# A last group of nodes with 312 columns in place of 384, in the last stage of a graph layer and its mixture of experts

## The chip, the cores and the metric

The kernel runs on one core of one Trainium2 chip. The metric is the device time of one execution in microseconds (us); lower is better. Five engines work side by side and meet at semaphores: TensorE (PE, its weight loads shown as PEld), VectorE (DVE), ScalarE (ACT), GpSimd (POOL) and SyncE (SP), which here only issues DMAs.

## The reference

3125 nodes with 256 features pass a graph attention layer with a feed-forward block, and then a mixture of 8 experts that all see every node. The parts that the change touches are these:

```python
h = _layernorm(x + x_new, ln1_g, ln1_b)
ffn = jax.nn.gelu(h @ W1 + b1, approximate=False) @ W2 + b2      # W1 256x1024, W2 1024x256
return _layernorm(h + ffn, ln2_g, ln2_b)
...
feat = jnp.mean(x, axis=0)                     # a mean over an axis of length 1
w = jax.nn.softmax(feat @ Wr + br, axis=-1)    # a weight for each node and expert
h = jnp.einsum('bfd,edh->bfeh', x, W1) + b1
h = jax.nn.relu(_bn(h, g1, be1, m1, v1))
h = jnp.einsum('bfeh,ehk->bfek', h, W2) + b2
h = jax.nn.relu(_bn(h, g2, be2, m2, v2))
y = jnp.einsum('bfeh,ehd->bfed', h, Wo) + bo
return jnp.einsum('bfed,fe->bfd', y, w)
```

## The kernel before

The program has three parts, run one after the other: `project` (keys, values, queries), `attend` (the graph attention, some 880 us of the span), and `tail` (line numbers from about 1040), which holds the feed-forward and the experts. Only `tail` is touched.

The nodes lie in NB = 25 blocks of BP = 128 rows. 24 blocks are full, and the last holds REST = 53 real nodes; its other rows are padding. `tail` takes the blocks in NC = 7 groups of CH = [3, 4, 4, 4, 4, 3, 3] blocks, numbered 0 to 6; group 6, the last, holds the partly filled block. A group of 4 blocks is 512 columns wide when the features lie on the partitions, a group of 3 blocks 384.

Each float32 product is made of three products of rounded float32 parts (type fp32r): high by low, low by high, high by high. With the contraction over 256 features in KC = 2 halves this is 6 matmuls for one 128-wide slice of the output. Two shapes of product occur:

- The nodes as the moving operand, the weights stationary. These are the feed-forward's first product (`hidden_first`, L1509, L1510, L1512: 8 slices `m` for each group, so 48 matmuls) and the experts' layers 1 and 2 (`layer`, L1554, L1555, L1557: 2 slices for each, so 12 matmuls for each layer, group and expert). They stream as many columns as the group has: `cols(g)`.
- The nodes stationary, the weights moving. These are the feed-forward's second product (`hidden_second`, L1532 to L1534), the experts' third layer (`third`, L1572, L1573, L1575), the bias product (`biases`, L1586 to L1588) and the router (`router`, L1485, L1488). They work block by block; the first three stream 256 columns, the router 16 or 8.

Behind each product with moving nodes stands a chain of three engines. ACT reads PSUM and applies Gelu (L1374, and L1375 for the rounded high part) or scale, bias and Relu (`hidden`, L1386); DVE makes the rounded high part in the experts' layers (L1786); POOL subtracts to get the low part (`gelu_low` L1279, `hidden_low` L1287). All of them work on `cols(g)` columns. PE needs the low part before it can use the result in the next product.

The order on each engine is written out by hand. In the experts' loop a step `i` from 0 to NJ - 1 = 55 is one expert and one group (`e, g = i // NC, i % NC`), and PE does `layer(1, i + 1)`, `layer(2, i)`, and then `third(i - 1)`, so that each chain has another step's products to hide behind. Some late work of the last group of the feed-forward is put between the steps (`LATE_X`, `LATE_R`), and the bias products of the 7 groups are spread over steps 9 to 15. DVE adds each expert's output, weighted, into the result (`combined`, L1801). The output of a group goes out by DMA (L1254, L1257) when its last expert is added.

Of the kernel before, what the change touches and what calls it, by code (L numbers as in the profile page):

```python
# [29 lines left out]
N, HID, E = 3125, 256, 53125  # L30
H, D = 4, 64
FF = 4 * HID
NB, BP = 25, 128
NPAD = NB * BP
FULL = N // BP
REST = N - FULL * BP
# [25 lines left out]
CH = [3, 4, 4, 4, 4, 3, 3]  # L62
NC = len(CH)
NPT = NC * FC
S_LAG = 2
NE = 8
XP = [(0, 4), (4, 12), (12, 20), (20, NB)]
EV = TP // 16 * 16
PARTS = [(0, REST // 16 * 16), (REST // 16 * 16, REST)]
SGRP = [(0, 4), (4, 8), (8, 12), (12, 16), (16, 20), (20, NB)]  # L70
KVB = 4
QEARLY = 9
# [18 lines left out]
def project(nc, ctx, io, keep):  # L91

    c = ExitStack()
    with c:
# [92 lines left out]
        def _(sp):  # L187
            def piece(k):
                a, b = XP[k]
                sp.dma_start(xs[:, a:min(b, FULL), :], x_v[:, a:min(b, FULL), :]).then_inc(s_x[k], 16)  # L190
                if b > FULL:
                    sp.wait_ge(s_pad, 3)
                    for a, b in PARTS:
                        sp.dma_start(xs[a:b, FULL, :], x_r[a:b, :]).then_inc(s_x[k], 16)
# [36 lines left out]
        def _(pool):  # L231
# [14 lines left out]
            def roots(k):  # L246
                a, b = SGRP[k]
                pool.wait_ge(s_mv, b)
                nc.gpsimd.tensor_scalar(ve[:, a:b], mv[:, a:b, 1], LN_EPS, None, ALU.add).then_inc(s_ve, 1)
                pool.wait_ge(s_ve, k + 1)  # L250
                nc.gpsimd.tensor_tensor(rs[:, a:b], ve[:, a:b], mh[:, a:b], ALU.pow).then_inc(s_rs, 1)
# [119 lines left out]
        def _(dve):  # L371
# [14 lines left out]
            def arrived(t):  # L386
                for k, (a, b) in enumerate(XP):
                    if t == a:
                        dve.wait_ge(s_x[k], 16 + 16 * len(PARTS) if b > FULL else 16)

            def norm(t):
                for k, (a, b) in enumerate(SGRP):
                    if t == a:
                        dve.wait_ge(s_rs, k + 1)
                if t >= 4:
                    dve.wait_ge(s_tr, t - 3)
                nc.vector.tensor_scalar(xn[:, t % 4, :], xs[:, t, :], mv[:, t, 0:1], rs[:, t:t + 1],
                                        ALU.subtract, ALU.mult).then_inc(s_xn, 1)
# [646 lines left out]
def tail(nc, ctx, io, keep):  # L1045

    c = ExitStack()
    with c:
        def sb(name, shape, dt=F32):
            return c.enter_context(nc.sbuf_tensor(name, shape, dt))  # L1050

        def pb(name, shape):
            return c.enter_context(nc.psum_tensor(name, shape, F32))
# [6 lines left out]
        xh = sb("xh", [P, KC, NPAD], F32R)  # L1060
        xl = sb("xl", [P, KC, NPAD], F32R)
# [37 lines left out]
        wrs = sb("wrs", [P, KC, 2 * NE], F32R)  # L1099
# [9 lines left out]
        psT = pb("psT2", [P, 512])  # L1109
# [23 lines left out]
        def size(g):  # L1133
            return CH[g]

        def first(g):
            return sum(CH[:g])

        def cols(g):
            return CH[g] * BP  # L1140

        def blocks(g):
            return slice(first(g), first(g) + size(g))
# [58 lines left out]
        def _(sp):  # L1202
# [5 lines left out]
            def inputs(g):  # L1208
# [4 lines left out]
                if g == NC - 1:  # L1213
                    for a, b in PARTS:
                        sp.dma_start(xin[a:b, full, :], x_r[a:b, :]).then_inc(s_xin, 16)
# [35 lines left out]
            for g in range(NC):  # L1251
# [3 lines left out]
                if g == NC - 1:  # L1255
                    for a, b in PARTS:
                        sp.dma_start(out_r[a:b, :], acc[a:b, NB - 1, 0:HID]).then_inc(s_out, 16)  # L1257
            sp.wait_ge(s_out, 16 * NC + 16 * len(PARTS))

# [184 lines left out]
        def _(pe):  # L1444
            def bank_free(use):

                n = t_at[use]
                if n:
                    before = T_USES[n - 1]
                    if before[0] in "TX":  # L1450
                        pe.wait_ge(s_th, tx_at[before] + 1)
                    else:
                        pe.wait_ge(s_pd, td_at[before] + 1)
# [23 lines left out]
            def router(g):  # L1477
                bank_free(("R", g))
                if g == 0:
                    pe.wait_ge(s_wrs, 4)  # L1480
                pe.wait_ge(s_tl, tx_at["X", g, KC - 1] + 1)
                for u in range(size(g)):
                    t = (first(g) + u) * BP
                    for k in range(KC):
                        nc.tensor.matmul(psT[:, 2 * NE * u:2 * NE * (u + 1)], xh[:, k, t:t + BP], wrs[:, k, :],  # L1485
                                         start=(k == 0), stop=False)
                    for k in range(KC):
                        last = nc.tensor.matmul(psT[:, 2 * NE * u:2 * NE * u + NE], xl[:, k, t:t + BP], wrs[:, k, 0:NE],  # L1488
                                                start=False, stop=(k == KC - 1))
                last.then_inc(s_pt, 1)  # L1490

# [68 lines left out]
            def third(i):  # L1560
                e, g = i // NC, i % NC
                pe.wait_ge(s_gl, low_at["L2", i, 1] + 1)
                if g == 0:
                    pe.wait_ge(s_wl, 3 * e + 3)
                hi, lo = half(e, 2, 0), half(e, 2, 1)
                for b, pair in enumerate(banks(g)):
                    ps = output_free(("L3", i, b))
                    for u in pair:
                        out = ps[:, (u % 2) * HID:(u % 2 + 1) * HID]
                        at = slice(u * BP, (u + 1) * BP)  # L1570
                        for k in range(KC):
                            nc.tensor.matmul(out, h2h[:, i % 2, k, at], lo[:, k, :], start=(k == 0), stop=False)  # L1572
                            nc.tensor.matmul(out, h2l[:, i % 2, k, at], hi[:, k, :], start=False, stop=False)  # L1573
                        for k in range(KC):
                            last = nc.tensor.matmul(out, h2h[:, i % 2, k, at], hi[:, k, :], start=False, stop=(k == KC - 1))  # L1575
                    last.then_inc(s_o, 1)

            def biases(g):

                pe.wait_ge(s_pd, td_at["wT", g] + 1)  # L1580
                for b, pair in enumerate(banks(g)):
                    ps = output_free(("bias", g, b))
                    for u in pair:
                        out = ps[:, (u % 2) * HID:(u % 2 + 1) * HID]
                        at = slice(u * BP, (u + 1) * BP)
                        nc.tensor.matmul(out, wTh[:, g % 2, at], bol[:, :], start=True, stop=False)  # L1586
                        nc.tensor.matmul(out, wTl[:, g % 2, at], boh[:, :], start=False, stop=False)
                        last = nc.tensor.matmul(out, wTh[:, g % 2, at], boh[:, :], start=False, stop=True)  # L1588
                    last.then_inc(s_o, 1)
# [14 lines left out]
            for p in range(NPT):  # L1604
                g, m = p // FC, p % FC
# [5 lines left out]
                if m == 4 and g == 1:  # L1611
                    bank_free(("sc",))
                    pe.wait_ge(s_sc, 6)
                    for k in range(4):
                        last = nc.tensor.transpose(psT[:, k * NP:(k + 1) * NP], sc[:, k, :], ident[0:NP, 0:NP])
# [28 lines left out]
        def _(dve):  # L1644
            def rows(t, n):
                return t[:, :].unsqueeze(1).broadcast_to([BP, n, HID])
# [54 lines left out]
            def second_stats(g):  # L1701
# [16 lines left out]
                last.then_inc(s_c2, 1)  # L1718
                dve.wait_ge(s_xin, 16 * g + 16 + (16 * len(PARTS) if g == NC - 1 else 0))
                nc.vector.tensor_tensor(xin[:, 0:n, :], xin[:, 0:n, :], rows(be2, n), ALU.add).then_inc(s_xb, 1)  # L1720
# [271 lines left out]
```

## Time and profile before

| | |
|---|---|
| time, median of 3 runs | 1502.57 us (1501.42 to 1509.48) |
| profiled execution, its own time | 1504.69 us |
| profiled execution, span from first to last instruction | 1502.9 us |
| mean granted TensorE clock over the span | 0.933 |
| PE, DVE, ACT, POOL busy over the span | 83%, 72%, 54%, 62% |

The span is 1.8 us shorter than the execution's own time, which also holds what lies around the first and the last instruction. The page cuts the span into 40 equal slices of 37.6 us; `tail` begins in the 24th. From the 29th slice on nearly every slice has the digit 9 for PE, that is 90% or more. A matmul's duration in the trace includes its way through the array, and overlaps the next one's: how fast PE gets on is read from the distance between the starts, not from the durations. Where the idle time of an engine is given, the arrow names what ended it.

### The profile page before, as it was taken

The numbers are of one execution on the slowest core, as the hardware profiler recorded it, in microseconds if no ns is written. First come the engines' busy times: TensorE is split into PE (matmuls) and PEld (weight loads), VectorE is DVE, ScalarE is ACT, GpSimd is POOL, SyncE is SP. The second block draws the span as 40 slices with busy tenths as digits, with TensorE's granted clock in tenths as the row PEclk, the third lists the DMA queues.
The fourth block names the chain that finished last, engine by engine and source line by source line (L and its number), as shares of the span: only waits on it lengthen the run. The fifth ranks groups of instructions, "written<-read, shape, count | busy, mean of one in ns | idle before, by whom it ended". The sixth has DMA issues, their size and how long they took to land. (4 is left out here: it accounts for less than half of the span.)

```text
span 1502.9 us, 24128 instructions
## 1 busy us (share of the span) xinstructions
PE 1247.5 (83%) x6835; PEld 966.9 (64%) x6835; DVE 1078.1 (72%) x2557; ACT 810.3 (54%) x2534; POOL 930.9 (62%) x883
## 2 busy tenths in 40 slices
PE   7988776677767677667657889999999999999998
PEld 3444454454445444444445578889898899999998
DVE  7647877777777787777868779886766665656655
ACT  1356766556666766566657654565543344444443
POOL 3365566656666665666665556866765477667765
PEclk9999879888898898998988999999999999999999
DMA  7477766666666666666665120101000000000002
GB/s 222 162 218 210 224 192 192 178 180 185 199 186 199 178 199 174 201 172 197 184 180 166 31 75 29 52 27 40 9 15 22 1 22 15 8 22 15 1 12 76
DMA packets 74072, 175.40 MB, mean 117 GB/s; under 512 B 11500, under 2 KB 36651, under 8 KB 73945
## 3 DMA queue, kind: packets, MB, share of 16 engines
q0 software_dynamic: 37632, 124.28, 29.6%
q1 hardware_dynamic: 34641, 48.25, 9.6%
q10 hardware_dynamic: 1672, 1.33, 0.3%
q8 instruction: 61, 1.00, 0.3%
q14 instruction: 66, 0.54, 0.1%
HBM read 159.91 MB, written 13.91 MB: 116 GB/s over the span
## 5 line engine op out<-in xcount | busy, mean ns | idle before, releaser
L690 POOL DMA_INDIRECT ring<-kv_rows,idx x464 | 466.5, 1005 | 296.4 <-issue 116.6
L764 ACT ACTIVATE ring<-ring 128x64 f32<-128x64 f32 x1800 | 442.1, 336 | 17.2 <-issue 16.1
L1287 POOL TENSOR_TENSOR wm<-k_gf,wm 128x512 fp32r<-128x512 f32 (+1 forms) x224 | 264.0, 1181 | 147.1 <-DVE wm L1786 147.1
L1386 ACT ACTIVATE k_gf<-psF,k_scT 128x512 f32<-128x512 f32 (+1 forms) x224 | 164.0, 733 | 258.3 <-PE psF L1557 258.3
L1786 DVE CAST wm<-k_gf 128x512 fp32r<-128x512 f32 (+1 forms) x224 | 168.8, 758 | 158.7 <-ACT k_gf L1386 157.0
L810 PE MATMUL psA<-ring,oh 128*128 128x260 f32 x912 | 274.1, 429 | 7.5 <-DVE k_acc L1016 7.1
L784 PE MATMUL psQ<-k_q,ohT 128*128 x1392 | 225.3, 304 | 58.7 <-issue 58.2
L982 DVE TENSOR_TENSOR prod<-psQ,ring 128x512 f32<-128x512 f32 x232 | 157.4, 678 | 89.5 <-remote 59.9
L784 PEld LDWEIGHTS psQ<-k_q,ohT 128*128 128x128 bf16 x1392 | 131.9, 105 | 115.7 <-issue 86.0
L810 PEld LDWEIGHTS psA<-ring,oh 128*128 128x128 f32 x912 | 178.0, 217 | 36.5 <-issue 8.5
L1022 DVE TENSOR_REDUCE alpha<-prod 128x8 f32<-128x512 f32 x232 | 155.6, 671 | 0.2
L1016 DVE TENSOR_TENSOR k_acc<-k_acc,psA 128x260 f32 x232 | 93.6, 403 | 15.4 <-PE psA L810 12.3
L1279 POOL TENSOR_TENSOR gT<-k_gf,gT 128x512 fp32r<-128x512 f32 (+1 forms) x56 | 74.1, 1325 | 38.8 <-ACT gT L1375 38.7
L1801 DVE SCALAR_TENSOR_TENSOR k_acc<-psO,wt,k_acc 128x256 f32<-128x256 f32 x200 | 84.8, 473 | 9.4 <-PE psO L1575 9.3
L1000 DVE TENSOR_TENSOR oh<-k_iotaF,k_dstR 128x256 f32<-128x256 f32 x217 | 88.3, 407 | 0.0
L1374 ACT ACTIVATE k_gf<-psF,b1c 128x512 f32<-128x512 f32 (+1 forms) x56 | 36.0, 642 | 77.3 <-PE psF L1512 77.2
L1532 PE MATMUL psO<-wm,gT 128*128 128x256 f32 x200 | 58.9, 294 | 0.0
L749 ACT ACTIVATE nrow<-psM 64x128 f32<-64x128 f32 x29 | 7.8, 270 | 93.4 <-remote 43.7
L1534 PE MATMUL psO<-wm,gT 128*128 128x256 f32 x200 | 57.0, 285 | 0.0
L1533 PE MATMUL psO<-wm,gT 128*128 128x256 f32 x200 | 56.9, 285 | 0.0
L846 PE MATMUL psA<-k_wqs,k_acc 128*128 128x512 f32 x100 | 49.3, 617 | 8.0 <-ACT qst L715 4.0
L755 ACT ACTIVATE ring<-dif 128x64 f32<-128x64 f32 x29 | 9.7, 334 | 85.6 <-DVE dif L961 60.8
(284 smaller groups left out, 2671.9 us busy)
## 6 DMA issues: line engine op xcount, KB each, us to landing
ohT<-step_destinations SPq DMA_DIRECT2D x29, 512.0 KB
ring<-kv_rows,idx POOLq DMA_INDIRECT x464
kv_rows<-kvst SPq DMA_DIRECT2D x25, 260.0 KB, 2.4
we<-in_L_ffn_W SPq DMA_DIRECT2D x16, 256.0 KB, 2.8
residual<-qst SPq DMA_DIRECT2D x25, 128.0 KB
xs<-in_x SPq DMA_DIRECT2D x2, 1024.0 KB, 8.8
resin<-residual SPq DMA_DIRECT2D x4, 512.0 KB
we<-in_L_ffn_Wo SPq DMA_DIRECT2D x8, 256.0 KB, 2.7
```

What stands on the lines that cost most here:

```text
L690: nc.gpsimd.indirect_dma_start(out=ring[:, LT * (j % CP) + k, j // CP:j // CP + 2, :].rearrange("p t e -> p (t e)"), out_offset=None, in_= ...
L764: last = nc.scalar.activation(row[:, 0:D], row[:, 0:D], ACT.Copy, scale=row[:, D:HW_])
L784: last = nc.tensor.matmul(psQ[j % NQ][:, k * HID:(k + 1) * HID], ohT[par][:, w * P:(w + 1) * P], q3[:, part, bass.ds(blk, 1), :].rearrange ...
L810: last = nc.tensor.matmul(psA[sj % NA][0:BP, 0:HALFW], onehot(b, k), ring[:, LT * (sj % CP) + k, sj // CP, :], start=(k == 0), stop=(k == ...
L982: nc.vector.tensor_tensor(prod[:, j % 2, :].rearrange("p (k d) -> p k d", k=LT), psQ[j % NQ][:, :].rearrange("p (k d) -> p k d", k=LT), ri ...
L1000: nc.vector.tensor_tensor(oh[:, sj % NO, :, :], iotaF[:, 0:BP].unsqueeze(1).broadcast_to([P, LT, BP]), dstR[:, bass.ds(LT * bo, LT)].unsqu ...
L1016: nc.vector.tensor_tensor(row, row, psA[sj % NA][0:BP, 0:HALFW], ALU.add).then_inc(s_acc, 1)
L1022: nc.vector.tensor_reduce(alpha[:, q % 2, :, LT * jj:LT * jj + LT].rearrange("p h w -> p w h"), prod[:, j % 2, :].rearrange("p (k h d) -> ...
L1287: nc.gpsimd.tensor_tensor(low[:, i % 2, m, 0:w], gf[:, n % 4, 0:w], high[:, i % 2, m, 0:w], ALU.subtract).then_inc(s_gl, 1)
L1386: nc.scalar.activation(gf[:, n % 4, 0:cols(g)], ps, ACT.Relu, bias=bias, scale=scale).then_inc(s_ev, 1)
L1786: nc.vector.tensor_copy((h1h if layer == 1 else h2h)[:, i % 2, m, 0:w], gf[:, n % 4, 0:w]).then_inc(s_dh, 1)
L1801: last = nc.vector.scalar_tensor_tensor(out=x1(t), in0=psO[n % 3][:, (u % 2) * HID:(u % 2 + 1) * HID], scalar=wt[:, t, e:e + 1], in1=x1(t) ...
```

## The change

The last group is narrower: its third block counts RC = 56 columns (53 rounded up to a multiple of 8) in place of 128, so `cols(6)` is 2 x 128 + 56 = 312 in place of 384, for every instruction that uses `cols(g)` on PE, ACT, DVE and POOL. In the router, the third layer and the bias product of the last block, 56 rows are stationary in place of 128, and 56 PSUM partitions are written. The feed-forward's second product still takes three blocks of 128 stationary rows, and the transposes, `combined` and the DMAs are as before.

```diff
--- before.py
+++ after.py
@@ -67,6 +67,7 @@
 XP = [(0, 4), (4, 12), (12, 20), (20, NB)]
 EV = TP // 16 * 16
 PARTS = [(0, REST // 16 * 16), (REST // 16 * 16, REST)]
+RC = -(-REST // 8) * 8
 SGRP = [(0, 4), (4, 8), (8, 12), (12, 16), (16, 20), (20, NB)]
 KVB = 4
 QEARLY = 9
@@ -1137,7 +1138,10 @@
             return sum(CH[:g])
 
         def cols(g):
-            return CH[g] * BP
+            return CH[g] * BP if g < NC - 1 else (CH[g] - 1) * BP + RC
+
+        def rows_in(g, u):
+            return RC if g == NC - 1 and u == CH[g] - 1 else BP
 
         def blocks(g):
             return slice(first(g), first(g) + size(g))
@@ -1480,12 +1484,12 @@
                     pe.wait_ge(s_wrs, 4)
                 pe.wait_ge(s_tl, tx_at["X", g, KC - 1] + 1)
                 for u in range(size(g)):
-                    t = (first(g) + u) * BP
+                    t, n = (first(g) + u) * BP, rows_in(g, u)
                     for k in range(KC):
-                        nc.tensor.matmul(psT[:, 2 * NE * u:2 * NE * (u + 1)], xh[:, k, t:t + BP], wrs[:, k, :],
+                        nc.tensor.matmul(psT[0:n, 2 * NE * u:2 * NE * (u + 1)], xh[:, k, t:t + n], wrs[:, k, :],
                                          start=(k == 0), stop=False)
                     for k in range(KC):
-                        last = nc.tensor.matmul(psT[:, 2 * NE * u:2 * NE * u + NE], xl[:, k, t:t + BP], wrs[:, k, 0:NE],
+                        last = nc.tensor.matmul(psT[0:n, 2 * NE * u:2 * NE * u + NE], xl[:, k, t:t + n], wrs[:, k, 0:NE],
                                                 start=False, stop=(k == KC - 1))
                 last.then_inc(s_pt, 1)
 
@@ -1566,8 +1570,9 @@
                 for b, pair in enumerate(banks(g)):
                     ps = output_free(("L3", i, b))
                     for u in pair:
-                        out = ps[:, (u % 2) * HID:(u % 2 + 1) * HID]
-                        at = slice(u * BP, (u + 1) * BP)
+                        n = rows_in(g, u)
+                        out = ps[0:n, (u % 2) * HID:(u % 2 + 1) * HID]
+                        at = slice(u * BP, u * BP + n)
                         for k in range(KC):
                             nc.tensor.matmul(out, h2h[:, i % 2, k, at], lo[:, k, :], start=(k == 0), stop=False)
                             nc.tensor.matmul(out, h2l[:, i % 2, k, at], hi[:, k, :], start=False, stop=False)
@@ -1581,8 +1586,9 @@
                 for b, pair in enumerate(banks(g)):
                     ps = output_free(("bias", g, b))
                     for u in pair:
-                        out = ps[:, (u % 2) * HID:(u % 2 + 1) * HID]
-                        at = slice(u * BP, (u + 1) * BP)
+                        n = rows_in(g, u)
+                        out = ps[0:n, (u % 2) * HID:(u % 2 + 1) * HID]
+                        at = slice(u * BP, u * BP + n)
                         nc.tensor.matmul(out, wTh[:, g % 2, at], bol[:, :], start=True, stop=False)
                         nc.tensor.matmul(out, wTl[:, g % 2, at], boh[:, :], start=False, stop=False)
                         last = nc.tensor.matmul(out, wTh[:, g % 2, at], boh[:, :], start=False, stop=True)
```

No instruction is added, removed or moved on any engine; on PE 240 instructions change from 384 to 312 columns (48 of the feed-forward, 192 of the experts), and 55 from 128 to 56 rows. The end of PE's program shows both. `psF` holds a layer's result, `wm` the activations, `gT` the weights, `psO` the output of the third layer; the piece is the second slice of layer 2 of the last step, and then the beginning and the end of what follows. Before:

```order
L1554 MATMUL psF<-wm,gT 128x384
L1555 MATMUL psF<-wm,gT 128x384
L1554 MATMUL psF<-wm,gT 128x384
L1555 MATMUL psF<-wm,gT 128x384
L1557 MATMUL psF<-wm,gT 128x384 x2
L1572 MATMUL psO<-gT,wm 128x256
...
L1572 MATMUL psO<-gT,wm 128x256
L1573 MATMUL psO<-gT,wm 128x256
L1575 MATMUL psO<-gT,wm 128x256 x2
```

The same rows after the change (lines are 4 to 5 further down in the file):

```order
L1558 MATMUL psF<-wm,gT 128x312
L1559 MATMUL psF<-wm,gT 128x312
L1558 MATMUL psF<-wm,gT 128x312
L1559 MATMUL psF<-wm,gT 128x312
L1561 MATMUL psF<-wm,gT 128x312 x2
L1577 MATMUL psO<-gT,wm 128x256
...
L1577 MATMUL psO<-gT,wm 56x256
L1578 MATMUL psO<-gT,wm 56x256
L1580 MATMUL psO<-gT,wm 56x256 x2
```

The places and the count are the same; only the moving width of the layer and the output rows of the last block differ.

## Rows read from the trace of the kernel before

**Rows 1.** The page: busy time by engine, and busy tenths in 40 slices.
```profile
PE 1247.5 (83%) x6835; PEld 966.9 (64%) x6835; DVE 1078.1 (72%) x2557; ACT 810.3 (54%) x2534; POOL 930.9 (62%) x883
PE   7988776677767677667657889999999999999998
```

**Rows 2.** Busy time by stretch: from:to, length, PE, PEld, DVE, ACT, POOL, clock, DMA.
```profile
1030.00:1051.50 21.50, 21.44 (x159) 21.04 (x158) 12.45 (x29) 12.52 (x25) 14.72 (x14) 1.00 0.15 44
1087.00:1091.00 4.00, 4.00 (x23) 4.00 (x23) 2.00 (x4) 2.22 (x5) 3.63 (x4) 0.61 0.02 8
1150.00:1156.00 6.00, 6.00 (x26) 5.46 (x25) 2.32 (x6) 1.44 (x3) 1.96 (x3) 0.72 0.16 44
1156.00:1200.00 44.00, 43.60 (x277) 39.39 (x276) 30.25 (x53) 13.38 (x19) 21.86 (x20) 1.00 0.03 7
1200.00:1494.00 294.00, 294.00 (x1789) 272.35 (x1788) 177.49 (x297) 122.88 (x172) 202.06 (x171) 1.00 0.06 18
```

**Rows 3.** PE in order of time, groups 5 and 6 of one expert: start, duration.
```profile
1328.02 0.34 PE L1554 MATMUL psF<-xh,ew 128*128 128x384 f32 x1
...
1332.19 0.28 PE L1572 MATMUL psO<-ew,wm 128*128 128x256 f32 x1
...
1335.06 0.34 PE L1554 MATMUL psF<-xh,gT 128*128 128x384 f32 x1
```

**Rows 4.** All engines in order of time, a stretch of 512 columns.
```profile
1462.11 0.39 PE L1554 MATMUL psF<-xh,gT 128*128 128x512 f32 x1
...
1466.19 0.28 PE L1572 MATMUL psO<-gT,wm 128*128 128x256 f32 x1
```

**Rows 5.** PE in order of time, the last group of the feed-forward, slices 1 and 2.
```profile
1032.30 0.34 PE L1509 MATMUL psF<-hT,wm 128*128 128x384 f32 x1
...
1034.41 0.34 PE L1509 MATMUL psF<-hT,wm 128*128 128x384 f32 x1
```

**Rows 6.** Waits after 1087 us: who for whom, us in total, times, longest.
```profile
PE psT L1474 <- ACT xn L1355: 3.6, 1, 3.6
PE psO L1572 <- POOL wm L1287: 0.4, 1, 0.4
```

**Rows 7.** All engines in order of time, the last step.
```profile
1494.44 0.67 ACT L1386 ACTIVATE k_gf<-psF,k_scT 128x384 f32<-128x384 f32 x1 [0.37 <-PE psF L1557]
1495.14 0.63 DVE L1786 CAST wm<-k_gf 128x384 fp32r<-128x384 f32 x1 [0.68 <-ACT k_gf L1386]
1495.86 1.01 POOL L1287 TENSOR_TENSOR wm<-k_gf,wm 128x384 fp32r<-128x384 f32 x1 [0.29 <-DVE wm L1786]
1496.15 0.40 PE L1575 MATMUL psO<-gT,wm 128*128 128x256 f32 x2
1496.92 0.39 PE L1572 MATMUL psO<-gT,wm 128*128 128x256 f32 x1 [0.38 <-POOL wm L1287]
```

**Rows 8.** Groups by line and shape after 800 us: busy us, mean ns, idle before.
```profile
L1287 POOL TENSOR_TENSOR wm<-k_gf,wm 128x512 fp32r<-128x512 f32 x128 | 166.6, 1303 | 88.1 <-DVE wm L1786 88.1
L1786 DVE CAST wm<-k_gf 128x512 fp32r<-128x512 f32 x128 | 101.6, 797 | 101.9 <-ACT k_gf L1386 101.9
L1386 ACT ACTIVATE k_gf<-psF,k_scT 128x512 f32<-128x512 f32 x128 | 99.6, 779 | 152.1 <-PE psF L1557 152.1
L1287 POOL TENSOR_TENSOR wm<-k_gf,wm 128x384 fp32r<-128x384 f32 x96 | 97.4, 1017 | 59.0 <-DVE wm L1786 59.0
L1786 DVE CAST wm<-k_gf 128x384 fp32r<-128x384 f32 x96 | 67.3, 706 | 56.8 <-ACT k_gf L1386 55.1
L1386 ACT ACTIVATE k_gf<-psF,k_scT 128x384 f32<-128x384 f32 x96 | 64.4, 672 | 106.2 <-PE psF L1557 106.2
```

**Rows 9.** PE in order of time, the router's last block of the last group.
```profile
1102.43 0.37 PE L1485 MATMUL psT<-wrs,xh 128*128 128x16 f32 x2
1102.65 0.36 PE L1488 MATMUL psT<-wrs,xl 128*128 128x8 f32 x2
1102.88 0.42 PE L1554 MATMUL psF<-wm,ew 128*128 128x384 f32 x1
```

## The prediction

> **What bounds the kernel now.** I read the page first. PE has the largest busy share, and its row of tenths is 9 in nearly every slice from the 29th on [rows 1]; before that no engine fills its slices, but the change touches nothing there. So I went to busy time by stretch. In the experts' steady part, 1200 to 1494 us, PE is busy 294.00 of 294.00 us at a granted clock of 1.00, while DVE has 177.49, ACT 122.88 and POOL 202.06 [rows 2]. In the stretch that holds the feed-forward's last group, 1030 to 1051.5 us, PE is busy 21.44 of 21.5 us, again at clock 1.00 [rows 2]. Both places in which the change shortens PE's work are bound by PE alone. The view of waits agrees: of PE's waits that end after 1087 us two matter here, 3.6 us before the transposes of the feed-forward's last group, which end at its left edge, and 0.4 us for POOL at the very end [rows 6].
>
> Since durations overlap, I took the price of a matmul from the distance of starts. Width 384: 24 matmuls from 1328.02 to 1332.19 us, 4.17 / 24 = 173.8 ns. Width 256: 24 from 1332.19 to 1335.06, 2.87 / 24 = 119.6 ns [rows 3]. Width 512: 18 from 1462.11 to 1466.19, 4.08 / 18 = 226.7 ns [rows 4]. The three lie on a line: 54.2 ns and 52.9 ns for 128 columns more, in the mean 0.418 ns for a column (one column in a cycle of the upper clock level, 2.4 GHz, would be 0.417), and about 13 ns that don't depend on the width.
>
> **The change part by part.**
>
> *Layers 1 and 2 of the experts, on PE.* 8 experts x 2 layers x 12 matmuls = 192, each 72 columns shorter: 72 x 0.418 = 30.1 ns, from 173.8 to 143.7 ns. Sum 5.78 us. The four-block and other three-block groups are unchanged.
>
> *First product of the feed-forward, on PE.* 48 matmuls x 30.1 ns = 1.44 us. Is it on the path? From one slice to the next are 1034.41 - 1032.30 = 2.11 us [rows 5]; 6 matmuls of 384 and 9 of 256 make 6 x 173.8 + 9 x 119.6 = 2.12 us. There is no gap, so all of it counts. ACT, DVE and POOL are busy 12.5, 12.5 and 14.7 of these 21.5 us [rows 2], and their pieces for this group shrink with PE's, so none becomes the bound.
>
> *The chain behind each product.* ACT, DVE and POOL shorten too: from 512 to 384 columns their means fall 107, 91 and 286 ns [rows 8], so 72 columns less are 60, 51 and 161 ns. In the loop this is worth nothing, because PE's other products hide the chain. It counts once: in the last step PE has only `third` of step 54 to hide behind, runs out of it, and waits. Its last two matmuls start at 1496.15, so the next could start at 1496.15 + 2 x 0.12 = 1496.39; it starts at 1496.92, behind ACT 0.67, DVE 0.63 and POOL 1.01 us [rows 7]. The stall of 0.53 us shrinks by 60 + 51 + 161 ns = 0.27 us, and 0.26 us stay. What is late next is still POOL's low part. Bounds: 0.16 us (POOL alone) to 0.53 us (the stall gone).
>
> *56 stationary rows in the router.* Here the moving operand has only 16 or 8 columns, and still the last block's 4 matmuls take from 1102.43 to 1102.88, 0.45 / 4 = 112 ns each [rows 9]: at such widths the weight load of 128 columns is the price. With 56 columns I take 112 x 56 / 128 = 49 ns, saving 4 x 63 = 0.25 us, once. No row shows a load of 56 columns; the bounds are 0 and 0.25 us, and I take 0.2, as it would scale with columns.
>
> *56 stationary rows in the third layer and the bias product.* 8 x 6 + 3 matmuls. Their start distance is 119.6 ns, above the 112 ns of a full load [rows 3, 9], so the moving 256 columns set it. I take 0. Below, if the 13 ns that don't depend on width belong to the load and scaled with its columns, 51 x 13 x 72 / 128 = 0.4 us would be saved; above, nothing suggests more than 0.1 us lost.
>
> *Everything else.* The transposes' copies, wT and the last group's Gelu pieces are shorter off the path. The wait of 3.6 us [rows 6] hangs on DVE and ACT work of 256 features for each block, which is unchanged; it moves with PE and stays as long.
>
> Sum: 5.78 + 1.44 + 0.27 + 0.20 = 7.7 us. Against the profiled execution's own time, 1504.69 us, this gives 1497.0 us. That execution lies 2.1 us above the median of the three runs, so against the median of 1502.57 us it gives 1494.9 us, 0.51% less.
>
> A rule of the Trainium skill speaks against this size: "TensorE: Matmul & The Clock Gate", section "Back-to-back issue gap", gives for a sustained stream of loads and matmuls about 81 ns at 128 columns and 131 ns at 512, so 0.13 ns for a column. By that rule 240 matmuls would save only 240 x 72 x 0.13 = 2.3 us as an estimate. The trace does not agree: 226.7 ns at 512 columns.
>
> **The rivals.**
>
> *The clock falls more often (the one on the other side).* PE's clock is granted by what PE has done. The trace has a stretch at the lower level, 1.2 GHz, that follows no long wait: 1150 to 1156 us has a mean clock of 0.72 [rows 2], behind bias products with few rows and transposes. It cost (1 - 0.72) x 6 = 1.7 us. If the third layer's last block, with 56 of 128 stationary columns, did the same after each pass of the last group, 8 x 1.7 = 13.4 us would be lost, and the time would be 1502.6 - 7.7 + 13.4 = 1508.3 us; with twice that for each pass, 1522. It decides from 7.7 / 1.7 = 5 passes on. For it: bias products are narrow in the array too. Against it: in the steady part, which holds such a block every seventh step, the clock is 1.00 throughout, the narrow part would be 6 matmuls or 0.7 us among hundreds at full size, and the later bias products, from 1156 to 1200 us, left the clock at 1.00 [rows 2].
>
> *Part of the gain is given back, or one low stretch more.* If the feed-forward's share were taken up by a wait for POOL's chain, 1.4 us less is won: 1496.4 us. One more stretch at the lower level (1.7 us) gives 1496.6 us, and both with the end's stall unchanged and the router's term at nothing 1494.9 + 1.4 + 1.7 + 0.5 = 1498.5 us. For it: after the long wait the clock is 0.61 for 4 us [rows 2], and where such a stretch falls depends on what stands around it, which moves by 1.4 us. Against it: ACT, DVE and POOL have 7 to 9 us of slack in 21.5.
>
> *One low stretch less.* By the same shift the stretch at 1150 us may fall away: 1494.9 - 1.7 = 1493.2 us.
>
> *Widths that are no multiple of 128 don't follow the line.* No row shows a width between 256 and 384 for these products. If 312 cost as much as 384, only the end and the router stay: 1502.1 us. If the cost for a column were much smaller there, as the rule above has it, 2.3 + 0.5 us are won: 1499.8 us. The three widths on one line, at one column in a cycle, speak against both.
>
> **How the numbers follow.** Chances: the forecast 0.71 (own range 1492.3 to 1497.5, which is one low stretch and the scatter of the medians), partly given back 0.14, one low stretch less 0.07, off the line 0.03, more low stretches 0.05. The time is that of the forecast, 1494.9 us. Eight in ten reach over the forecast's range and most of the two cases beside it: 1491.2 to 1499.6 us. About 0.5% (7.5 us) is what a measurement of this kernel can tell from no change, and the forecast lies just past this line, so it is split: 0.45 of its 0.71 is beyond it, 0.26 within. Faster by over 0.5%: 0.45 + 0.07 = 0.52. Within 0.5%: 0.26 + 0.14 + 0.03, and 0.02 of the slower rival at one stretch a pass, makes 0.45. Slower by over 0.5%: 0.03.
>
> **What the profile of the changed kernel would show.** The step of one expert is shorter by 24 x 30 ns = 0.72 us every 7 steps; width 312 has a start distance of 144 ns. From slice to slice in the feed-forward's last group are 1.94 us. The last stall of PE is near 0.3 us. The router's last 4 matmuls come at about 50 ns. PE's busy share from 1200 us on stays at all of it, at clock 1.00. The prediction is wrong if that distance is not 144 ns, if PE begins to wait in the loop for POOL or DVE, or if the mean clock behind the passes of the last group falls below 1.00.

## The result, and the profile after

| | before | changed |
|---|---|---|
| median, 9 runs each | 1502.57 us (1498.76 to 1509.48) | 1492.04 us (1487.78 to 1499.95) |
| ratio of the runs | | 0.9947 (0.9924 to 0.9969) |
| profiled execution, its own time | 1504.69 us | 1499.95 us |
| its span | 1502.9 us | 1498.1 us |

The forecast was 1494.9 us with a ratio of 0.995. The median of 1492.04 us lies 0.3 us below the forecast's own range (1492.3 to 1497.5) and inside the wider one (1491.2 to 1499.6). Two later comparisons, each of 12 runs of the changed kernel with 23 and 19 of the kernel before, gave 0.9951 (0.9916 to 0.9985) and 0.9937 (0.9914 to 0.9960).

The times scatter by some 20 us, and the traces say where: before the part that was changed (three traces of the changed kernel come into it at 1014.64, 1024.46 and 1035.40 us, and take 458.9 to 459.0 us from there). The stretch that the change touches runs from the first matmul of the feed-forward's last group to the last matmul of the program. I call it the tail below; it is only the last part of what the function `tail` does. In the kernel before, PE in order of time (start, duration) at its two ends:

```profile
1030.12 0.38 PE L1509 MATMUL psF<-hT,wm 128*128 128x384 f32 x1
...
1498.94 0.40 PE L1575 MATMUL psO<-gT,wm 128*128 128x256 f32 x2
```

The last matmul of the pair starts at 1499.06, so the tail is 468.94 us. The same for the changed kernel:

```profile
1035.40 0.31 PE L1513 MATMUL psF<-hT,wm 128*128 128x312 f32 x1
...
1494.20 0.40 PE L1580 MATMUL psO<-gT,wm 128*56 128x256 f32 x2
```

Its last matmul starts at 1494.32: 458.92 us. The tail is 10.0 us shorter, while this execution came into it 5.3 us later, by work that no edit touched. So the trace shows the change a good deal more sharply than the times do. 10.0 us are a ratio of 0.9933, inside all three intervals.

Busy time by stretch in the changed kernel (from:to, length, PE, PEld, DVE, ACT, POOL, clock, DMA), to compare with [rows 2]:

```profile
1035.00:1056.50 21.50, 21.30 (x167) 21.01 (x166) 11.67 (x29) 11.83 (x26) 13.95 (x15) 1.00 0.18 52
1090.70:1095.00 4.30, 4.30 (x26) 4.30 (x27) 2.22 (x4) 2.31 (x5) 3.94 (x5) 0.67 0.05 18
1152.00:1158.00 6.00, 5.93 (x33) 5.20 (x33) 3.56 (x8) 2.02 (x3) 2.77 (x3) 1.00 0.13 44
1158.00:1200.00 42.00, 42.00 (x275) 37.98 (x275) 28.91 (x53) 12.55 (x19) 21.39 (x20) 1.00 0.03 7
1200.00:1487.00 287.00, 287.00 (x1769) 265.40 (x1769) 168.96 (x294) 120.92 (x171) 197.50 (x170) 1.00 0.06 18
```

PE is still the only bound in the steady part. What is new is the third row: the stretch with a clock of 0.72 that stood at 1150 us in [rows 2] is not there. The widths themselves, in PE's order of time, beside [rows 3]:

```profile
1335.19 0.30 PE L1558 MATMUL psF<-wm,ew 128*128 128x312 f32 x1
...
1336.90 0.28 PE L1577 MATMUL psO<-ew,wm 128*128 128x256 f32 x1
```

12 matmuls in 1.71 us are 142.5 ns each; the forecast was 143.7. The router's last block, beside [rows 9]:

```profile
1105.99 0.25 PE L1489 MATMUL psT<-wrs,xh 128*56 128x16 f32 x2
1106.09 0.24 PE L1492 MATMUL psT<-wrs,xl 128*56 128x8 f32 x2
1106.19 0.42 PE L1558 MATMUL psF<-wm,ew 128*128 128x384 f32 x1
```

4 matmuls in 0.20 us, 50 ns each in place of 112. And the last step, beside [rows 7]:

```profile
1489.97 0.61 ACT L1390 ACTIVATE k_gf<-psF,k_scT 128x312 f32<-128x312 f32 x1 [0.24 <-PE psF L1561]
1490.62 0.59 DVE L1792 CAST wm<-k_gf 128x312 fp32r<-128x312 f32 x1 [0.53 <-ACT k_gf L1390]
1491.29 0.85 POOL L1291 TENSOR_TENSOR wm<-k_gf,wm 128x312 fp32r<-128x312 f32 x1 [0.26 <-DVE wm L1792]
1491.69 0.40 PE L1580 MATMUL psO<-gT,wm 128*128 128x256 f32 x2
1492.19 0.38 PE L1577 MATMUL psO<-gT,wm 128*128 128x256 f32 x1
```

From 1491.69 + 0.24 = 1491.93 to 1492.19 PE stalls for 0.26 us; before it was 0.53.

Every instruction has the same place in both programs, so the tails can be laid side by side, matmul by matmul. A low stretch is one in which the granted clock is at its lower level. This is where the 10.0 us come from:

| part of the tail | forecast | measured |
|---|---|---|
| experts' layers 1 and 2, width | 5.78 | 5.68 |
| feed-forward's first product, width | 1.44 | 1.42 |
| router, 56 rows | 0.20 | 0.24 |
| end of the last chain | 0.27 | 0.28 |
| low stretch near 1150 us gone | a rival, 1.7 | 1.54 |
| waits and starts in the bias products | 0 | 0.87 |
| sum | 7.7 | 10.03 |

### The profile page after: what moved, and what is told of

Same layout as the page of the kernel before. It is cut to its first block and busy times, and to the rows that moved or that the text cites. A ratio compares the mean times of both kernels' runs of the same rounds, so it can differ in the third digit from the quotient of the medians.

```text
span 1498.1 us, 24128 instructions
## 1 busy us (share of the span) xinstructions
PE 1242.9 (83%) x6835; PEld 959.2 (64%) x6835; DVE 1068.4 (71%) x2557; ACT 807.4 (54%) x2534; POOL 927.2 (62%) x883
## 5 line engine op out<-in xcount | busy, mean ns | idle before, releaser
L1291 POOL TENSOR_TENSOR wm<-k_gf,wm 128x512 fp32r<-128x512 f32 (+2 forms) x224 | 258.9, 1159 | 144.1 <-DVE wm L1792 144.1
L1390 ACT ACTIVATE k_gf<-psF,k_scT 128x512 f32<-128x512 f32 (+2 forms) x224 | 162.1, 724 | 252.2 <-PE psF L1561 248.9
L785 PE MATMUL psQ<-k_q,ohT 128*128 x1392 | 228.6, 305 | 60.7 <-issue 56.0
L1792 DVE CAST wm<-k_gf 128x512 fp32r<-128x512 f32 (+2 forms) x224 | 159.5, 719 | 155.8 <-ACT k_gf L1390 155.8
L1283 POOL TENSOR_TENSOR gT<-k_gf,gT 128x512 fp32r<-128x512 f32 (+2 forms) x56 | 73.3, 1310 | 38.2 <-ACT gT L1379 38.1
L1378 ACT ACTIVATE k_gf<-psF,b1c 128x512 f32<-128x512 f32 (+2 forms) x56 | 35.5, 634 | 76.9 <-PE psF L1516 76.8
L1578 PE MATMUL psO<-ew,wm 128*128 128x256 f32 (+1 forms) x200 | 52.9, 286 | 0.0
```

The lines of the kernel that those rows point to most:

```text
L785: last = nc.tensor.matmul(psQ[j % NQ][:, k * HID:(k + 1) * HID], ohT[par][:, w * P:(w + 1) * P], q3[:, part, bass.ds(blk, 1), :].rearrange ...
L1291: nc.gpsimd.tensor_tensor(low[:, i % 2, m, 0:w], gf[:, n % 4, 0:w], high[:, i % 2, m, 0:w], ALU.subtract).then_inc(s_gl, 1)
L1390: nc.scalar.activation(gf[:, n % 4, 0:cols(g)], ps, ACT.Relu, bias=bias, scale=scale).then_inc(s_ev, 1)
L1792: nc.vector.tensor_copy((h1h if layer == 1 else h2h)[:, i % 2, m, 0:w], gf[:, n % 4, 0:w]).then_inc(s_dh, 1)
```

## The experiments

Length of the tail in every profiled kernel, in us. Where a low stretch stands near the bias products, the last column says how far behind the start of the tail it begins. w192 and third_56_all leave out a part of the result.

| kernel | tail | low stretch near the bias products |
|---|---|---|
| before, first / again | 468.94 / 468.93 | at 121.4 / at 149.6 |
| changed, first / again / third | 458.92 / 458.92 / 458.99 | no / no / no |
| rows_only | 468.47 | at 121.3 |
| pe_only | 460.52 | no |
| experts_only | 460.20 | no |
| ffn_only | 469.19 | at 121.7 |
| third_56_all | 459.22 | at 118.1 |
| early_norm | 462.78 | at 121.7 |
| early_norm_late_router | 460.04 | no |
| w192 | 454.96 | no |
| rc54 | 458.77 | no |

### before_again and after_again: what is scatter

No edit.

> The kernel before once more, as a control for the scatter. Theory (the gain is the width on PE, the rest is scatter): ratio to the kernel before 1.000 with an interval of about 0.3% to either side; in the trace the same start distances (173.8 ns at 384 columns) and the end's stall of 0.53 us, but the stretches at the lower clock may lie elsewhere, one more or less (1.7 us each) behind 1026 us. Rival (the low stretch at 1150 us belongs to the kernel before): a low stretch at 1145 to 1160 us again.

Measured: ratio to the kernel before 1.0002 (0.9975 to 1.0030). The tail is the same to 0.01 us, though this execution came into it 16 us earlier. The low stretch is there again, but behind another bias product, 28 us further on. Busy time by stretch and, below it, the bias product just before it, all engines in order of time:

```profile
1163.00:1169.00 6.00, 6.00 (x23) 4.94 (x22) 1.69 (x4) 1.70 (x3) 1.28 (x1) 0.72 0.01 3
```

```profile
1159.16 1.02 POOL L1287 TENSOR_TENSOR wm<-k_gf,wm 128x384 fp32r<-128x384 f32 x1 [0.30 <-DVE wm L1786]
1159.23 1.17 DVE L1786 CAST wm<-k_gf 128x384 fp32r<-128x384 f32 x1
...
1160.89 0.55 DVE L1821 TENSOR_TENSOR hT<-psT,hT 8x384 fp32r<-8x384 f32 x1
1160.89 0.38 PE L1586 MATMUL psO<-bol,hT 8*128 8x256 f32 x1
...
1161.36 1.25 DVE L1801 SCALAR_TENSOR_TENSOR k_acc<-psO,wt,k_acc 128x256 f32<-128x256 f32 x3
...
1162.27 0.38 PE L1586 MATMUL psO<-bol,hT 8*128 8x256 f32 x1 [0.40 <-DVE k_acc L1801]
```

The second row is the one to look at. DVE's cast of 384 columns lasts 1.17 us here, where 0.36 us is its shortest; it began 0.07 us after POOL's subtraction and ended only behind it. DVE is thereby late with adding the expert's output, which frees the bank that the bias product waits for. That is the 0.4 us wait of PE (0.66 us with the slower start behind it). In the first trace of the kernel before the same cast lasts 1.16 us and the wait is the same, but the low stretch begins 28 us ahead of the wait: the two need not go together.

> The changed kernel once more. Theory: ratio 0.995 (7.7 us), interval about 0.992 to 0.998; in the trace from the feed-forward's last group on, the same 30 ns for each of 240 matmuls, and low stretches behind the feed-forward at places that differ from the first trace's. Rival (the change itself takes away the low stretch at 1150 us): none there again, and a ratio nearer 0.994.

Measured: 0.9951 (0.9916 to 0.9985), tail 458.92 us, no low stretch near the bias products. So the rival's sign came and the ratio was the theory's, though an interval this wide cannot part 0.995 from 0.994. At the same place in the changed kernel's first trace:

```profile
1176.27 1.00 POOL L1291 TENSOR_TENSOR wm<-k_gf,wm 128x384 fp32r<-128x384 f32 x1 [0.30 <-DVE wm L1792]
1176.35 1.33 DVE L1792 CAST wm<-k_gf 128x312 fp32r<-128x312 f32 x2 [0.16 <-ACT k_gf L1390]
...
1177.54 1.68 POOL L1291 TENSOR_TENSOR wm<-k_gf,wm 128x312 fp32r<-128x312 f32 x2 [0.26 <-DVE wm L1792]
...
1178.66 1.24 DVE L1807 SCALAR_TENSOR_TENSOR k_acc<-psO,wt,k_acc 128x256 f32<-128x256 f32 x3
...
1178.94 0.38 PE L1592 MATMUL psO<-bol,hT 8*128 8x256 f32 x1
```

Two casts now begin before POOL's next subtraction. The first is still held until the subtraction beside it ends (1.10 us), and the second begins in the gap between two of them and takes 0.31 us. DVE starts its adding 0.28 us before the bias product's first matmul (1178.94) instead of 0.47 us behind it (1161.36 against 1160.89), and the wait is gone. Shorter casts are not needed for that: in pe_only they have 384 columns and the wait is gone too. What counts is when they begin.

### rows_only: the 56 rows alone

```diff
         def cols(g):
-            return CH[g] * BP if g < NC - 1 else (CH[g] - 1) * BP + RC
+            return CH[g] * BP
```

> Only the rows: 384 columns everywhere as before, but 56 stationary rows for the last block in the router, the third layer and the bias product. Theory: the router's last 4 matmuls fall from 112 to about 50 ns (0.25 us in all), the third layer's last 6 stay at 119 to 120 ns, nothing else moves; the time is within 0.5 us of the kernel before, scatter aside. Rival (narrow products lower the clock): low stretches appear after passes of the last group, 1.7 us each, up to 13 us.

Measured: tail 468.47 us, 0.47 less than before. The router gives 0.24 of it, matmuls at 50 ns; the rest lies in single intervals under 0.1 us. No low stretch is added behind the passes of the last group; the one near the bias products stays. The rival on the other side has nothing to stand on here.

### pe_only: the helpers keep 384 columns

```diff
         def cols(g):
+            return CH[g] * BP
+
+        def pcols(g):
             return CH[g] * BP if g < NC - 1 else (CH[g] - 1) * BP + RC
...
-                    h1h[:, i % 2, :, 0:cols(g)], h1l[:, i % 2, :, 0:cols(g)])
+                    h1h[:, i % 2, :, 0:pcols(g)], h1l[:, i % 2, :, 0:pcols(g)])
...
-                    ps = product_free(f_at[f"L{l}", i, m])[:, 0:cols(g)]
+                    ps = product_free(f_at[f"L{l}", i, m])[:, 0:pcols(g)]
```

Likewise in `hidden_first`.

> 312 columns on PE alone; ACT, DVE and POOL still work on 384 of them (the last 72 are left over from other work and used by nobody that is kept). Theory: the whole of the layers' gain, 24 x 30 = 0.72 us for each expert and 8 x 6 x 30 = 1.44 us in the feed-forward, but the stall at the end stays at about 0.53 us instead of 0.27. Rival (the helpers' shorter work carries part of the gain): the step of one expert shrinks by clearly less than 0.7 us, as PE begins to wait for ACT or POOL in the loop.

Measured: tail 460.52 us, 1.60 more than the changed kernel. In the experts' loop the intervals are the changed kernel's to some hundredths of a us, but for those around the long wait, so the helpers carry nothing there. The end's last interval is 0.45 us longer (forecast 0.27). The rest, 1.2 us, is lost in the feed-forward's last group, which I had not expected. Waits from 1010 to 1060 us (who for whom, us in total, times, longest):

```profile
PE psT L1495 <- POOL xl L1284: 1.0, 1, 1.0
PEld psF L1519 <- ACT gT L1385: 0.6, 1, 0.6
PE psF L1519 <- POOL hT L1284: 0.5, 1, 0.5
PEld psO L1542 <- POOL gT L1289: 0.4, 1, 0.4
```

PE waits for ACT and POOL there. (The two waits at L1519 end with the tail's first matmul and are not in its length.) The helpers' 384 columns need not be the cause. In twelve of the fourteen traces a low stretch slows PE in the 20 us ahead of the tail. pe_only and early_norm_late_router alone have none, and they alone wait for POOL's low part before the router here for more than 0.23 us: 1.0 us, and 0.6 us with the helpers at 312 columns. Busy time by stretch for those 20 us, in pe_only and in the changed kernel:

```profile
990.80:1010.80 20.00, 18.22 (x134) 17.63 (x135) 17.81 (x39) 10.80 (x23) 15.10 (x12) 1.00 0.00 1
```

```profile
1015.40:1035.40 20.00, 18.90 (x130) 18.45 (x129) 15.61 (x42) 9.46 (x21) 13.46 (x13) 0.91 0.08 21
```

So a PE that was not slowed comes to this group ahead of its helpers. That this makes most of the 1.2 us is argued from two traces, and the helpers' widths may add to it: this stays open.

### experts_only and ffn_only: the two halves

`cols(g)` is split into one for the feed-forward and one for the experts; one of them is 384 for the last group.

```diff
+        def fcols(g):
+            return CH[g] * BP
...
-                x0, x1 = hTh[:, g % 2, :, 0:cols(g)], hTl[:, g % 2, :, 0:cols(g)]
+                x0, x1 = hTh[:, g % 2, :, 0:fcols(g)], hTl[:, g % 2, :, 0:fcols(g)]
```

> 312 columns in the experts alone; the feed-forward's first product and its helpers keep 384. Measured from the start of the feed-forward's last group to the last matmul (468.94 us in the kernel before, 458.92 us in the changed one). Theory (each part counts by itself, and the bias product's wait and the low stretch near it belong to the experts' widths): 458.92 + 1.4 = 460.3 us, no wait of 0.66 us in the bias product, no low stretch there. Rival (the low stretch is chance, by the phase of the clock's grid): it comes back, 461.9 us.

> 312 columns in the feed-forward's first product alone; the experts keep 384 and all 128 rows. Same stretch. Theory: 468.94 - 1.4 = 467.5 us, with the bias product's wait of 0.66 us and a low stretch near the bias products as in the kernel before. Rival (chance): the low stretch is gone here too, 465.9 us.

Measured: experts_only 460.20 us, against 460.3, with neither the bias product's wait nor a low stretch. The feed-forward's first product alone is 1.44 us longer than in the changed kernel. ffn_only took 469.19 us against 467.5: the 1.4 us are there in the intervals, the wait of 0.66 us and the stretch near the bias products are back, and one more low stretch fell behind the router of group 4. Busy time by stretch of ffn_only:

```profile
906.00:912.00 6.00, 6.00 (x39) 6.00 (x39) 3.37 (x13) 1.22 (x3) 2.34 (x3) 0.72 0.64 183
1011.90:1017.90 6.00, 6.00 (x25) 5.38 (x24) 2.08 (x5) 1.64 (x3) 2.02 (x2) 0.72 0.15 44
```

The two halves are additive in their widths. What the experts' half brings beyond its widths is the wait. For the stretch one trace of each is not enough, as the next run shows.

### third_56_all: is the clock or the load sensitive to narrow products?

```diff
-                        n = rows_in(g, u)
+                        n = RC
                         out = ps[0:n, (u % 2) * HID:(u % 2 + 1) * HID]
```

in the third layer, for every block.

> The changed kernel, but in the experts' third layer every block has only 56 stationary rows, so that 72 rows of each block get no expert output. Theory (the moving 256 columns set the distance, and the clock doesn't look at how much of the array is used): 120 ns a matmul, clock 1.00 in the experts' steady part, 458.9 us. Rival (narrow products lower the clock): a third of PE's time now goes to narrow products, so the clock falls in the loop, by 1.7 us for each stretch; the stretch takes clearly over 460 us. A second rival (part of the 13 ns that no width explains belongs to the weight load): 112 to 116 ns, up to 8 us less over 1200 matmuls.

Measured: tail 459.22 us. PE in order of time, 24 narrow matmuls, and the steady part by stretch:

```profile
1180.18 0.28 PE L1577 MATMUL psO<-ew,wm 128*56 128x256 f32 x1
...
1183.04 0.34 PE L1558 MATMUL psF<-xh,gT 128*128 128x384 f32 x1
```

```profile
1050.00:1340.00 290.00, 290.00 (x1797) 266.27 (x1795) 170.98 (x298) 122.12 (x173) 198.95 (x172) 1.00 0.06 18
```

2.86 / 24 = 119.2 ns, against 119.6 ns with 128 rows, and a clock of 1.00 over 290 us in which these matmuls are near a third of PE's time. The first rival falls, and of the second's up to 8 us little is left. But not nothing: the tail holds one low stretch (1.5 us) that the changed kernel has not, and is only 0.3 us longer. The third layer's distances add up to 1.5 us less in all; in the steady part they are 0.7 ns shorter in the mean. The low stretch stands where it stood in the kernel before, though the wide groups and the bias product's wait of 0.66 us are not there.

### w192 and rc54: other widths

w192 works on 192 columns in `layer` on PE, by the edit of pe_only with 192 in place of 312 and for the experts alone, with 384 for the helpers. rc54 has 310 columns throughout:

```diff
-RC = -(-REST // 8) * 8
+RC = REST + REST % 2
```

> 192 columns in the experts' layers 1 and 2 of the last group, on PE alone; the helpers work on 384, so the columns from 192 on get left-over values. Theory (a weight load of 128 columns costs 112 ns, the router's distance in the kernel before, and can't be hidden behind less): 112 ns a matmul, not the 93.6 ns of the line through the three widths. Rival 1 (the line goes on): 93 to 94 ns. Rival 2 (narrow moving operands cost more for this type below 256 columns): clearly over 120 ns.

> The last block with 54 rows in place of 56, 310 columns. Theory (the line holds for any width): 240 x 2 x 0.418 ns = 0.20 us less than the changed kernel's 458.92, so 458.7 us, chance stretches aside. Rival (56 was chosen because other counts cost more): 143 ns a matmul or more and no gain, or DVE's casts slower than 0.36 us.

Measured in w192, PE in order of time:

```profile
1318.30 0.25 PE L1564 MATMUL psF<-wm,ew 128*128 128x192 f32 x1
...
1319.62 0.31 PE L1583 MATMUL psO<-ew,wm 128*128 128x256 f32 x1
```

1.32 / 12 = 110 ns, not the 93.6 ns of the line and not over 120: the load of 128 columns sets the distance. By an estimate from these distances the line ends where it meets 110 ns, at about 256 - (119.6 - 110) / 0.418 = 233 columns.

rc54: tail 458.77 us, 0.15 less than the changed kernel, with 0.20 expected. But the saving is not in the matmuls that became narrower. In the steady part the 24 of one expert take 1.724 + 1.711 = 3.435 us at 310 columns and 1.712 + 1.717 = 3.429 us at 312, 143 ns each in both. What is shorter is layer 2 of group 5, which follows the first twelve of them at an unchanged 384 columns: 2.083 us in place of 2.115 (2.080 in the kernel before). This is also why the table above has 5.68 us for the experts' layers: the 192 matmuls themselves save 5.93 us, and the neighbours behind them give 0.25 us back. So two columns are less than this measurement resolves, and the rival's 143 ns is what came. 54 rows are as good as 56, and no better than can be told in a time.

### early_norm, early_norm_late_router and after_third: the long wait

The changed kernel still has the 3.6 us wait [rows 6] and a low stretch behind it.

```diff
-                if i in (1, 2):
-                    root(i, NC - 1)
+                if i in (0, 1):
+                    root(i + 1, NC - 1)
...
-                if i == 1:
+                if i == 0:
                     second_stats(NC - 1)
-                if i == 2:
+                if i == 1:
                     second_norm(NC - 1)
```

> The changed kernel with the second normalisation of the feed-forward's last group one step earlier in the experts' loop on DVE and POOL (statistics in step 0, normalisation in step 1). Theory (PE's wait of 3.6 us before the transposes in step 3 and the low stretch behind it hang on DVE's order): the wait goes, and with it the low stretch, 3.6 + 1.6 = 5.2 us, so 458.9 - 5.2 = 453.7 us, ratio to the kernel before 0.991 or less. Rival (DVE is late with the experts' outputs instead, and PE waits for a free bank in steps 1 and 2): less than 2 us are won.

Measured: ratio 0.9945 (0.9930 to 0.9961), tail 462.78 us, 3.9 more than the changed kernel. The wait of 3.6 us is gone, and another is there (waits, as above):

```profile
PE psT L1489 <- POOL xl L1278: 2.7, 1, 2.7
```

All engines in order of time show why: POOL's subtraction for group 5 lasts 3.19 us, in place of some 1.0, as it stands among DVE's normalisation:

```profile
921.57 3.19 POOL L1278 TENSOR_TENSOR xl<-tf,xh 128x384 fp32r<-128x384 f32 x1
...
922.46 1.43 DVE L1792 CAST wm<-k_gf 128x512 fp32r<-128x512 f32 x4
...
923.81 4.07 DVE L1734 SCALAR_TENSOR_TENSOR k_acc<-k_acc,rs,xin 128x256 f32<-128x256 f32 x3
```

Behind the new wait the clock is at 0.57 from 928 to 936 us, longer than before. Two more low stretches that the changed kernel has not stand in this tail, at 901 and at 1007 us (about 1.6 us each), so most of the 3.9 us is the clock and not the wait. Neither my theory nor the rival's place was right: the wait moved from ACT's chain to POOL's. The next kernel gives POOL a step more there:

```diff
-LATE_R = {2: NC - 2, 5: NC - 1}
+LATE_R = {3: NC - 2, 5: NC - 1}
```

> The changed kernel with the second normalisation of the last group one step earlier, as in early_norm, and the router of group 5 one step later (step 3 in place of 2), so that POOL's low part of that group's features, which PE waited for there, has a step more. Theory (each of the two waits is set by an order, none by an engine's load): neither the 3.6 us wait in step 3 nor the 2.7 us wait in step 2, and no low stretch behind them; from the feed-forward's last group to the end 458.9 - 3.6 - 1.6 = 453.7 us, one chance stretch more at most (455.3); ratio to the kernel before about 0.990. Rival (DVE and POOL have no room for this work in steps 0 to 3, and the wait turns up at a third place): 457 us or more.

> The changed kernel a third time, beside the version above on the same chip. Theory: 458.92 us from the feed-forward's last group to the end again (or one chance stretch more, 460.5), ratio to the kernel before 0.993 to 0.997: 10.0 us of the tail less a share of scatter of the earlier parts. Rival (the low stretch near the bias products is the old kernel's alone): never 460.5.

Measured: early_norm_late_router 0.9940 (0.9918 to 0.9961), tail 460.04 us; the changed kernel beside it 0.9937 (0.9914 to 0.9960), tail 458.99 us with no stretch near the bias products. For early_norm_late_router the rival holds. The wait turned up at a third place, the transposes of the last group behind the router's result:

```profile
PE psT L1478 <- DVE lg L1765: 2.5, 1, 2.5
PE psF L1558 <- POOL wm L1291: 1.5, 1, 1.5
```

A second new wait, for POOL's low part in the loop, costs 1.5 us more, and three smaller ones 1.5 us together. No low stretch stands in this tail at all, not even behind these waits.

Neither order beats the changed kernel.

## Why the prediction was right, and what it missed

- **PE alone bounds both places: right.** experts_only and ffn_only bring their widths' price each, and in the loop the intervals of pe_only are those of the changed kernel. The signs of being wrong did not come: 142.5 ns for 144, no wait in the loop, clock 1.00 behind the passes of the last group from 1158 us on.
- **30.1 ns for 72 columns, 240 times: right.** 5.68 + 1.42 = 7.10 us of 7.22. The price from three widths held at 312 and at 310 to 1 ns or so. The Trainium skill's two figures in "TensorE: Matmul & The Clock Gate", "Back-to-back issue gap", 81 ns at 128 columns and 131 ns at 512, make 0.13 ns for a column, and by that an estimate of 2.3 us. The runs do not agree with these figures: 142.5 ns at 312 columns against 173.8 at 384 is 0.43 ns for a column.
- **The end of the last chain: right**, 0.28 for 0.27 us. With the helpers at 384 columns the last interval is 0.45 us longer, so the shorter helpers are what shortens it.
- **56 rows in the router, nothing in the third layer: right.** 50 ns (forecast 49). With 56 rows in every block the distance was 119.2 ns in place of 119.6, so at most about 1 ns of the fixed 13 goes with the load's columns: over the 51 matmuls of this change that is under 0.1 us, with 0.4 us as the bound below.
- **"Everything else": this step failed.** I held the rest of the path unchanged. The bias product's wait was in [rows 2] as 43.60 of 44.00 us busy, and the view of waits of the kernel before had a row for it that [rows 6] and my "two matter here" left out:

```profile
PE psO L1586 <- DVE k_acc L1801: 0.4, 1, 0.4
```

  It hung on whether a cast of DVE begins just before or just behind a subtraction of POOL, and the change moved that. The wait and the slower start behind it make 0.66 of the 0.87 us; the rest is in single starts of about 0.1 us or less.
- **The low stretch: a rival with a chance of 0.07 that came true, 1.54 us, and by luck of place as far as the traces tell.** Of the kernels with 384 columns in the experts, four traces of four have a stretch near the bias products. Of those with 312, 310 or 192 and no other edit to rows or order, seven of seven have none. That looks as if the change took it away, with the bias product's wait as the reason. The places speak against it. The wait ends 148 to 150 us into the tail. In before, rows_only and ffn_only the stretch begins some 28 us ahead of it, and third_56_all and early_norm have a stretch at that earlier place and no such wait. Only in before_again does it stand behind the wait.
- **What parts the traces is the place against the clock's grid.** In the clock record of each trace the level changes only at points of an even grid, and the grid stands differently against the program in every execution. Ahead of the earlier place stands a step's first bias product, at 1148.62 us in the kernel before. It starts 0.14 to 1.24 us behind a grid point in the five traces with a stretch there, and 1.43 to 3.10 us behind one in the nine without. The change brings it from 118.5 to 116.2 us into the tail, and its three traces stand at 1.43 to 1.57 us. That is the prediction's own reason for this rival: where such a stretch falls depends on what stands around it. The limits are read off afterwards, with the nearest traces 0.2 us apart, and no run moves the grid alone: this is argued, not shown, and how often the changed kernel is spared the stretch is open.
- **The slower rival: refuted** by rows_only and third_56_all: no low stretch behind the passes of the last group, and clock 1.00 over 290 us with 56 rows in every block.

So the four terms of the forecast were right to 0.1 us, and 2.4 us came on top that it held fixed or gave little chance. The time itself, 2.9 us below the forecast, cannot tell 7.7 from 10.0 us: the ratio's interval is 0.45% wide, 6.8 us. The tail's length in the trace can.

## What to carry to other kernels

Where one engine is busy without a gap at full clock, price an edit by the distance between starts at two or three sizes, and count the instructions: the sum over the widths came out within 2%. Then look for waits of a few tenths of a us along that path that hang on two other engines' relative timing, and for stretches at half the clock, since these are what such a sum leaves out. Before a stretch that is gone is put down to an edit, look where it stood in each trace: here it stood at two places, and at one of them with and without the edit. And if a time scatters by more than the effect, find a stretch of the trace that holds all the edits and compare its length: here it repeated to 0.1 us while the times moved by 20.

## What the runs showed of the hardware that was not expected

- A DVE cast that begins during a POOL subtraction ends only behind it (1.17 us in place of 0.36). Of the experts' casts in the kernel before, 151 begin so, and 150 of them end 0.2 to 0.3 us behind the subtraction. In one place (early_norm) POOL's subtraction stretches from 1.0 to 3.19 us beside DVE's casts and normalisation.
- A weight load of 56 columns allows a distance of 50 ns between matmuls with 16 or 8 moving columns, one of 128 columns 112 ns; a load of 128 columns holds 192 moving columns to 110 ns.
- The parts ahead of the tail took 1010 to 1035 us in ten of the traces and 885 to 892 us in the other four (experts_only, ffn_only, third_56_all, early_norm), which were taken on another chip. The tail, bound by PE, did not differ: experts_only, one of the four, is 1.28 us above the changed kernel, and its edit alone accounts for 1.4. Busy time by stretch for the first 885 us, the changed kernel and experts_only:

```profile
0.00:885.00 885.00, 645.17 (x3061) 410.76 (x3061) 657.49 (x1774) 534.66 (x2100) 514.70 (x534) 0.89 0.62 182
```

```profile
0.00:885.00 885.00, 729.65 (x3990) 502.13 (x3991) 778.62 (x2040) 609.40 (x2248) 619.10 (x619) 0.98 0.64 188
```

In the same time the second got 3990 matmuls done in place of 3061, at a clock of 0.98 in place of 0.89. What makes the difference is open; no run was made for it.
